# A two-layer graph network on one Trainium2 core: six slots of gathered rows instead of four, given back by TensorE, and products 256 columns wide instead of 128

## The reference

```python
h = jnp.maximum(_layernorm(x, axis=-1), 0.0)
x = x + _L0_gnn_ref(h, edge_index, edge_attr_64, ...)   # layer 0
h = jnp.maximum(_layernorm(x, axis=-1), 0.0)
x = x + _L1_gnn_ref(h, edge_index, W, b, a_src, a_trg)  # layer 1

# layer 0: 6250 nodes x 256, 100000 edges sorted by dst, and a self loop for each node
e = jax.nn.relu(ea @ ee_w1 + ee_b1) @ ee_w2 + ee_b2     # ea: 64 columns per edge
agg = jax.ops.segment_sum(x[src] + e, dst, num_segments=n)
h = (1.0 + eps) * x + agg
h = relu(_ln(h @ w1 + b1, g1, be1)); h = relu(_ln(h @ w2 + b2, g2, be2))   # 1024 wide
out = relu(_ln(x + h @ w3 + b3, bn_g, bn_b))

# layer 1: attention over the same edges and self loops, 8 heads of 32
h_prime = (x @ W + b).reshape(n, 8, 32)
e = leaky_relu(h_src[src] + h_trg[trg]); exp_e = exp(e - max(e))
alpha = exp_e / (segment_sum(exp_e, trg)[trg] + 1e-10)
out = segment_sum(h_prime[src] * alpha[:, :, None], trg)
```

## Time and profile before

| | us |
|---|---|
| median of three runs | 3407.08 |
| the profiled execution | 3410.1 |
| its span | 3408.2 |
| busy: TensorE / VectorE / ScalarE / GpSimd | 2566.7 / 2285.9 / 1454.7 / 1992.3 |
| mean granted TensorE clock | 0.887 of 2.4 GHz |

### The profile page before, as it was taken

How to read it: one execution, slowest core, us unless ns; L and a number is a source line. 1 busy time by engine, 2 the same in 40 slices (tenths; PEclk the granted TensorE clock), 3 DMA queues, 4 the chain that set the end, 5 groups by cost and what they waited for, 6 DMA issues and landing times. The chain is left out here.

```text
span 3408.2 us, 97011 instructions
## 1 busy us (share of the span) xinstructions
PE 2566.7 (75%) x33058; PEld 2437.6 (72%) x33059; DVE 2285.9 (67%) x4707; ACT 1454.7 (43%) x3683; POOL 1992.3 (58%) x2153
## 2 busy tenths in 40 slices
PE   0577777777677758999999999994777777777773
PEld 0567666677676658999999999984776766776762
DVE  8677777777766744666666666665776766766676
ACT  5334434443333436777777777772111111111110
POOL 3666667776666633334443333333777777777774
PEclk9978888888887869999999999996888888888786
DMA  5545555554444420000000000002555655555554
GB/s 137 155 138 148 145 143 150 151 151 137 141 140 133 137 75 9 19 18 18 18 18 18 19 19 18 18 19 90 170 175 172 174 169 172 173 171 174 169 176 117
DMA packets 185718, 374.52 MB, mean 110 GB/s; under 512 B 43924, under 2 KB 95514, under 8 KB 185598
## 3 DMA queue, kind: packets, MB, share of 16 engines
q0 software_dynamic: 75552, 209.66, 22.1%
q1 hardware_dynamic: 107954, 162.91, 15.8%
q10 hardware_dynamic: 2092, 0.74, 0.1%
HBM read 347.36 MB, written 25.80 MB: 109 GB/s over the span
## 5 line engine op out<-in xcount | busy, mean ns | idle before, releaser
L450 POOL DMA_INDIRECT rows<-tab_scratch,idx x784 | 763.0, 973 | 355.9 <-issue 221.2
L1451 POOL DMA_INDIRECT a_rows<-tab_scratch,a_srcs x784 | 749.3, 956 | 240.9 <-issue 233.3
L1518 PE MATMUL sum_ps<-feat,a_hot 128*125 128x132 f32 x3920 | 609.0, 321 | 237.2 <-DVE feat L1611 124.6
L1518 PEld LDWEIGHTS sum_ps<-feat,a_hot 128*125 128x125 f32 x3920 | 565.9, 225 | 255.6 <-DVE feat L1611 135.7
L905 PE MATMUL z_ps<-ah,w 128*128 128x125 f16 x6400 | 554.9, 219 | 2.7 <-PEq L981 0.6
L905 PE MATMUL z_ps<-al,w 128*128 128x125 f16 x3200 | 543.8, 218 | 0.0
L905 PEld LDWEIGHTS z_ps<-ah,w 128*128 128x128 f16 x6400 | 490.5, 97 | 7.4 <-issue 7.3
L515 PE MATMUL sum_ps<-rows,hot 128*125 128x128 f16 x1960 | 370.5, 241 | 126.0 <-PEq L548 118.4
L505 PE MATMUL mlp_ps<-ewa,eab 128*128 128x128 f16 x1576 | 235.0, 238 | 284.2 <-PEq L500 283.1
L1461 ACT ACTIVATE feat<-d 128x32 f32<-128x32 f32 x196 | 45.0, 229 | 827.5 <-DVE d L1607 578.8
L482 ACT ACTIVATE rh<-mlp_ps 128x1024 f16<-128x1024 f32 x196 | 199.2, 1016 | 448.8 <-ACTq L481 420.5
(11 more groups left out here) (208 smaller groups left out, 5985.8 us busy)
## 6 DMA issues: line engine op xcount, KB each, us to landing
ea<-edge_t SPq DMA_DIRECT2D x394, 128.0 KB
dstb<-dst_flat SPq DMA_DIRECT2D x98, 512.0 KB
rows<-tab_scratch,idx POOLq DMA_INDIRECT x784
a_rows<-tab_scratch,a_srcs POOLq DMA_INDIRECT x784
tab_scratch<-prow SPq DMA_DIRECT2D x50, 128.9 KB
hx<-x SPq DMA_DIRECT2D x50, 125.0 KB
x_scratch<-x SPq DMA_DIRECT2D x50, 125.0 KB
hs<-tab_scratch SPq DMA_DIRECT2D x50, 125.0 KB
```

Source lines behind the costliest of these rows:

```text
L450: pool.indirect_dma_start(rows[:, s, k, :], None, dram["tab0"], bass.IndirectOffsetOnAxis(ap=idx[:, s, k:k + 1], axis=0),).then_inc(rows_r ...
L1451: pool.indirect_dma_start(rows[:, b % DEEP, k, :], None, dram["tab1"], bass.IndirectOffsetOnAxis(ap=srcs[:, c:c + 1], axis=0),).then_inc(r ...
L1518: ins = pe.matmul(out[:, c], hot[:, h, k, :], feat[:, row, k, c], start=(k == 0 and c is NARROW[0]), stop=(k == CB - 1 and c is NARROW[-1] ...
```

## The change

In `edges0` the ring of `rows` gets six slots. GpSimd's gathers are written out for all batches; they read their indices straight from `srcs`, which now lies in the memory of `st` (used in later stages only), and wait for `rows_free` with a rising count, which TensorE raises after its sums. The tile `idx`, VectorE's copies into it, its wait for `rows_free` and the semaphores `idx_ready` go. TensorE's loop takes six batches a turn, with the last four after the loop. The products of `edge_mlp` and `sums` have 256 columns, half as many instructions. VectorE's loop stays at four batches a turn; four increments of `lines` stand ahead of it in place of ten. In `edges1` alone TensorE's sums change: 264 columns instead of 132.

```diff
@@ edges0
-        srcs = m.sb("srcs", [P, NCH], I32)
+        srcs = sb["st"][:].rearrange("p t c -> p (t c)").bitcast(I32)
-        idx = m.sb("idx", [P, RING, CB], I32)
+        DEEP = 6
+        FULL, REST = divmod(NB, DEEP)
-        rows = m.sb("rows", [P, RING, CB, 2 * D], F16)
+        rows = m.sb("rows", [P, DEEP, CB, 2 * D], F16)
@@ gpsimd
-            with pool.Fori(0, NB // RING):
-                for s in range(RING):
-                    pool.wait_ge(idx_ready[s], 1)
-                    pool.sem_inc(idx_ready[s], -1)
-                    for k in range(CB):
-                        pool.indirect_dma_start(
-                            rows[:, s, k, :], None, dram["tab0"],
-                            bass.IndirectOffsetOnAxis(ap=idx[:, s, k:k + 1], axis=0),
-                        ).then_inc(rows_ready[s], 16)
+            pool.wait_ge(ld_idx, 16)
+            for b in range(NB):
+                if b >= DEEP:
+                    pool.wait_ge(rows_free, b - DEEP + 1)
+                for k in range(CB):
+                    c = CB * b + k
+                    pool.indirect_dma_start(
+                        rows[:, b % DEEP, k, :], None, dram["tab0"],
+                        bass.IndirectOffsetOnAxis(ap=srcs[:, c:c + 1], axis=0),
+                    ).then_inc(rows_ready[b % DEEP], 16)
@@ tensor
-                    for c in NARROW:
-                        pe.matmul(mlp_ps[:, s, k, c], eab[:, s, e], ewa[:, c], start=True, stop=False)
-                        ins = pe.matmul(mlp_ps[:, s, k, c], eah[:, s, e], ewb[:, c], start=False, stop=True)
+                    pe.matmul(mlp_ps[:, s, k, :], eab[:, s, e], ewa[:], start=True, stop=False)
+                    ins = pe.matmul(mlp_ps[:, s, k, :], eah[:, s, e], ewb[:], start=False, stop=True)
...
-            with pe.Fori(0, NB // RING) as i:
-                tiles = tiles_of(nc, PE, table, RING * i, RING)
-                for u in range(RING):
+            with pe.Fori(0, FULL) as i:
+                tiles = tiles_of(nc, PE, table, DEEP * i, DEEP)
+                for u in range(DEEP):
+                    body(tiles, i, u)
+            tiles = tiles_of(nc, PE, table, DEEP * FULL, REST)
+            for u in range(REST):
+                body(tiles, FULL, u)
@@ vector
-                dve.wait_ge(rows_free, 1)
-                dve.sem_inc(rows_free, -1)
-                indices(b - 1 + RING, ring)
-            dve.wait_ge(ld_idx, 16)
-            for b in range(RING):
-                indices(b, b)
-            for _ in range(10):
+            for _ in range(4):
                 dve.sem_inc(lines, 1)
@@ edges1, tensor
-                    for c in NARROW:
-                        ins = pe.matmul(out[:, c], hot[:, h, k, :], feat[:, row, k, c], start=(k == 0 and c is NARROW[0]),
-                                        stop=(k == CB - 1 and c is NARROW[-1]), skip_group_check=True)
+                    ins = pe.matmul(out[:], hot[:, h, k, :], feat[:, row, k, :], start=(k == 0), stop=(k == CB - 1))
```

More of the change, by code:

```diff
@@ L346, in edges0 @@
         acc, iota16, negbase, ewa, ewb = sb["acc"], sb["iota16"], sb["negbase"], sb["ewa"], sb["ewb"]
-        srcs = m.sb("srcs", [P, NCH], I32)
+        srcs = sb["st"][:].rearrange("p t c -> p (t c)").bitcast(I32)
+        assert NT * 2 * HEADS == NCH
         dsts = m.sb("dsts", [P, NCH + CB], F32)
-        idx = m.sb("idx", [P, RING, CB], I32)
+        DEEP = 6
+        FULL, REST = divmod(NB, DEEP)
         table = m.sb("table0", [1, 2, NBP + 4], I32)
-        rows = m.sb("rows", [P, RING, CB, 2 * D], F16)
+        rows = m.sb("rows", [P, DEEP, CB, 2 * D], F16)
         ea = m.sb("ea", [P, 2, BE], F32)
@@ L362, in edges0 @@
         wmean = m.sb("wmean", [P, WROWS], F32)
-        NARROW = [slice(c, c + D // 2) for c in (0, D // 2)]
         TURNS = (NB // RING - 1) // WROWS
@@ L372, in edges0 @@
         ld_tab = m.sem("ld_tab")
-        idx_ready = [m.sem(f"idx_ready{s}") for s in range(RING)]
-        rows_ready = [m.sem(f"rows_ready{s}") for s in range(RING)]
+        rows_ready = [m.sem(f"rows_ready{s}") for s in range(DEEP)]
         ea_ready = [m.sem(f"ea_ready{s}") for s in range(2)]
@@ L406, in _ @@
         def _(sp):
-            sp.dma_start(srcs[:], t["src_cols"]).then_inc(ld_idx, 16)
+            sp.dma_start(srcs, t["src_cols"]).then_inc(ld_idx, 16)
             sp.dma_start(table[:, :, 0:NBP + 1], dram["sched"][:, 0:NBP + 1].unsqueeze(0)).then_inc(ld_tab, 16)
@@ L511, in sums @@
                     lhs = hot[:, h, k, :]
-                    for c in NARROW:
[L513 to L521, removed]
+                    pe.matmul(out[:, 0:D], lhs, rows[:, ring, k, 0:D], start=(k == 0), stop=False, skip_group_check=True)
+                    pe.matmul(out[:, 0:D], lhs, rows[:, ring, k, D:2 * D], start=False, stop=False, skip_group_check=True)
+                    pe.matmul(out[:, D:2 * D], lhs, rh[:, s, k, :], start=False, stop=False, skip_group_check=True)
+                    ins = pe.matmul(out[:, D:2 * D], lhs, rl[:, s, k, :], start=False, stop=(k == CB - 1), skip_group_check=True)
                 return ins
@@ new lines, in body @@
+            def body(tiles, i, u):
+                s = u % 2
+                edge_mlp(1 - s)
+                lo, end = tiles[u]
+                pe.wait_ge(hot_ready, 1)
+                pe.sem_inc(hot_ready, -1)
+                pe.wait_ge(sum_free, 1)
+                pe.sem_inc(sum_free, -1)
+                pe.wait_ge(r_split, 1)
+                pe.sem_inc(r_split, -1)
+                pe.wait_ge(rows_ready[u], 16 * CB * (i + 1))
+                sums(sum_ps[:, s, :], s, u, s).then_inc(sum_done, 1)
+                with pe.If(end > lo + 1):
+                    with pe.Fori(lo + 1, end):
+                        pe.wait_ge(xhot_ready, 1)
+                        pe.sem_inc(xhot_ready, -1)
+                        sums(sum_ps[:, 2, :], 2, u, s).then_inc(xsum_done, 1)
+                pe.matmul(used_ps[:], ewa[:, 0:1], ewa[:, 0:1], start=True, stop=True).then_inc(r_free, 1)
+                pe.matmul(used_ps[:], ewa[:, 0:1], ewa[:, 0:1], start=True, stop=True).then_inc(rows_free, 1)
@@ L568, in add @@
                 dve.tensor_tensor(a, a, sum_ps[:, s, :], ALU.add).then_inc(sum_free, 1)
-            def main_hot(b, row, lo):
-                one_hot16(dve, hot[:, row], iota16, dsts, negbase, b, lo)
             def extra_hot(b, x):
@@ L582, in add_extra @@
                 dve.sem_inc(x_chain, -1)
-            def indices(b, s):
-                dve.tensor_copy(idx[:, s, :], srcs[:, bass.ds(CB * b, CB)]).then_inc(idx_ready[s], 1)
             def main_hot(b, s, lo):
@@ L596, in low_activations, with advance @@
                                          op0=ALU.max, op1=ALU.subtract).then_inc(r_split, 1)
-            def advance(b, s, ring, lo, end, following):
+            def advance(b, s, lo, end, following):
                 with dve.If(end > lo + 1):
@@ L641, in turn @@
                     if u or not isinstance(i, int):
-                        advance(b, s, (u - 1) % RING, *tiles[u], tiles[u + 2][0])
+                        advance(b, s, *tiles[u], tiles[u + 2][0])
                     else:
@@ L1320, in edges1 @@
         TC = 2 * HEADS
-        NARROW = [slice(c, c + TW // 2) for c in (0, TW // 2)]
         PAIR = RING // 2
```

## The result

The changed kernel takes 3331.62 us (median of four runs, 3327.83 to 3337.43) against 3407.2 us for the kernel before on the same chip: 0.9783 of it, 95% interval 0.9771 to 0.9796. That is 76 us less. Foretold were 3278 us and a range of 3264 to 3320, so the sign was right and the time lies outside the range. The profiled execution has a span of 3327.0 us.

A forecast was written before the change was run, and what follows sets the result against it. It took the chain of TensorE and VectorE to bound `edges0`, losing at row turns; afterwards the gathers would: 105.4 + 987.8 = 1093.2 us, plus a 7 us tail, ends at 1100, 131 us earlier, so 3278 us; range 3264 to 3320.

The forecast's parts named there:

- The start: GpSimd's first gather in `edges0` needs nothing of VectorE and starts at about 105.4 us, not 109.08: 3.7 us.
- The gathers: The 784 gathers of `edges0` take 987.8 us, as in `edges1`; bounds 977 and 1113.7 us.
- The ordinary turn: Four batches without row turn on TensorE and VectorE in `edges0`: from 19.6 to 17.6 us, between 15.4 and 19.2.
- the products' 0.6: Pairing 112 products into 256 columns on TensorE saves 0.6 us a turn, between 0 and 1.1.
- The copies' 0.3: VectorE's four dropped copies and a wait save 0.3 us a turn; bounds 0 and 1.
- TensorE's head: Idle time at TensorE's loop start falls from 2.06 to 1.5 us for six batches, saving 1.1 us a turn.
- The row turn: VectorE's idle time at each of 12 row turns in `edges0`: gain put at 0, up to 6.9 us each.
- The tail: From the last gather of `edges0` to the stage's end: 7 us, between 4 and 8; before 8.0.
- the chain as the bound: Rival: TensorE and VectorE still set the pace of `edges0`; 3292 to 3351 us, chance 0.23.
- Its middle case: Half of the savings on TensorE and VectorE: a turn of 18.4 us, four turns 83.5, time 3312 us.
- Slots without time: Rival: the change gives back slots but only the 3.7 us of the start: 3403 us, chance 0.03.
- The slower rival: VectorE's moved inner loop pays up to 6.9 us in each turn: about 3525 us, chance 0.04.

The follow-up runs named there:

- e8b: Kernel before with 16 increments of `lines` in place of 10 and products of 256 columns in `edges0` alone: 3320.6 us, ratio 0.9757.
- e1: Kernel before with 16 increments of `lines` in place of 10 ahead of VectorE's loop, nothing else: 3346.9 us, ratio 0.9850.
- e4b: Changed kernel with four slots in place of six and TensorE's turns of four batches: 3305.9 us, ratio 0.9716.
- e2: Changed kernel with no increment of `lines` in place of 4, so VectorE's outer loop begins 4 places earlier: 3328.9 us.
- e10b: Changed kernel with 18 increments of `lines` in place of four: 3378.0 us, ratio 0.9925.
- e12b: Changed kernel, still six slots, with a TensorE loop of 12 batches that loads tile bounds every four batches: 3307.0 us, ratio 0.9719.
- e4: Changed kernel with four slots and TensorE's turns of four batches, on a chip where the kernel before takes 4455 us: ratio 0.9143.

## Why the prediction was wrong, by its steps

The step that failed is the ordinary turn of the chain of TensorE and VectorE: put at 17.6 us, below the gathers' 20.2, and measured at 20.5. So the chain stayed the bound. The gathers' term failed beside it.

- The start: 105.2 us for the first gather, 105.4 foretold. Right.
- The gathers, 987.8 us, the sum's largest term: too small. The changed kernel takes 1027.0 us from the first to the last. 16 of the 39 us too many are the gathers' own, 765.4 us busy against 749.3, and 23 are waits above the usual 0.3 us. Both busy times stood in the earlier trace rows, 763.16 for this stage and 749.26 for `edges1`; I took the rate of the wrong stage. With this stage's own it is 784 x (0.973 + 0.30) = 998 us. The 16 us alone would have made 3294 us, within the range; the late chain took the time out of it.
- The ordinary turn, 19.6 to 17.6 us: the start was too low and the savings too high. The 19.6 was one turn; the mean of 36 is 20.9. After, the mean is 20.5: 0.4 us less, where 2.0 were foretold.
- Of its savings, the products' 0.6 was near: TensorE is busy for 32 us less in e8b than in e1, 0.65 us a turn, a part of it by the clock. The turn itself fell by 0.43 us, shorter heads included; in e8b rows are waited for. The copies' 0.3 was near too: e8b to e4b gives 0.4, though that holds the written-out gathers as well.
- TensorE's head was mis-sized. I foretold that it falls from 2.06 to 1.5 us for six batches, a gain of 1.1 us a turn of four. Measured is a median of 2.46 us where both engines have a head (with the small products; 2.34 without). The lead of wide products is real but 0.65 us, not 1.06 (median head 2.18 in e1, 1.53 in e4b). And each load of six values takes 1.467 us and not 1.2, so the two add 0.93 us and not 0.4: 1.53 + 0.93 = 2.46. I had taken the price of a value, 0.1 us, from VectorE's loads; on TensorE it is 0.23. Worse, I counted a head of six batches as if it replaced one and a half of four. It does not, since VectorE keeps its heads at every fourth batch. 93 us of idle time stand at heads where TensorE's 28 heads outside row turns were to cost 28 x 1.5 = 42.
- The row turn, gain put at 0 with up to 6.9: measured 5.35 us (28.58 to 23.23). The idle 4.65 us of the earlier trace rows are gone, the 2.28 are not. The Trainium skill's Runtime: NRT & Kernel Launch, section Instruction fetch mechanics, says that code comes in blocks of 256 instructions and that a jump out of the two blocks held waits for a fetch. The runs agree with that, with 92 and 98 packets where the loop touches three blocks and 38 and 43 where it touches two, but not with the places that I counted: by 513 to 806, e2's loop would have touched a third block, and it didn't. I should have taken this term. It made the result as good as it is, and as I had put it at nothing, that was luck: without it, by e10b, the time is 3378.
- The tail: 7 us foretold, 17 measured, since the chain is late.
- `edges1`: cost 0 foretold; its gathers take 989.4 us, before 987.8.

The sum for the stage: foretold to end at 1100, it ended at 1149.1. That is 16 (gathers' own) + 23 (waits) + 10 (tail) = 49 us. On the chain four turns take 23.2 + 3 x 20.5 = 84.8 us, 80.3 foretold: 4 x (20.5 - 17.6) = 11.7 too many for the ordinary turns, 7.2 too few for the row turn (2.7 above an ordinary one, not 7.9 + 2.0). Two errors in part cancelled.

Of the rivals, the chain as the bound was what happened. It had 0.23 for 3292 to 3351 us, and the range cut it at 3320. Its middle case says half of the savings and takes 18.4 us; half of the 2.0 us makes a turn of 18.6, so four turns of 84.3, 1033 us and a time of 3322 in place of 3312, outside the range already. Its four turns are near the 84.8 measured, though with 20.5 and 23.2 us in place of 18.6 and 28.5, so that too is two errors against each other. Slots without time was half right: the slots give no time, as e12b shows, but the rest of the change does. The slower rival, a fetch in each turn, didn't happen; a fetch in each row turn was in the kernel before, and e10b puts it back at 46 us. The 264 columns of `edges1` alone were not run.

## What to carry to other kernels

When two engines walk the same batches in loops of their own, keep the heads of the loops at the same batches: here 28 heads of TensorE, rarer but 16 of them out of step, came with VectorE's own to 93 us of idle time, and 36 heads in step to 53. Take the pace of a stage from the stage's own busy time, and a turn from the mean of many. Before a gain is put down to an edit, look at the packets of the instruction queue: here six instructions that do no work moved the time by 53 us.

## What the runs showed of the hardware

- A load of six values takes TensorE's queue 1.467 us and VectorE's 0.81; of four values TensorE's takes 1.000.
- An indirect gather of the same size takes 0.976 us in the mean in `edges0` of the changed kernel and 0.958 in `edges1`; the longest there took 1.89 and 1.24 us.
- Two of the chips ran the kernel before in 4455 and 4462 us in place of 3400 to 3407. In e4 the gather stages took 36 and 39% longer than in e4b, with gathers (0.964 us in the mean against 0.986) and activations (1.02 us) of the usual duration and late semaphores between engines.
